# A gated recurrence over two layers on one core: two full-precision products made of rounded halves, span states in one group, work placed anew

## What is computed

```python
# layer 0
h = relu(x @ w1[lang] + b1[lang])                    # (1024, 128)
x = x + layernorm(x + h @ w2[lang] + b2[lang]) * gamma0[lang] + beta0[lang]
# layer 1
ctx    = causal_ema(x, tau_ctx)                      # h_t = alpha h_(t-1) + x_t
gated  = x * sigmoid(concat(x, ctx) @ Wg.T + bg)     # 1024 columns in, 512 out
h1     = gelu(x @ Wn1.T + bn1)
mod    = 0.5 + sigmoid(h1 @ Wn2.T + bn2)             # 8 values for each time step
traces = [causal_ema(gated * mod[..., d], tau_raws[d]) for d in range(8)]
temporal = sum_d traces[d] * softmax(blend)[d]
gate   = sigmoid(temporal @ Wtemp.T + btemp)
soma   = gelu(x @ Wsoma.T + bsoma)
x = x + layernorm((soma * gate) @ Wout.T) * gamma + beta
```

## Time and profile before

| | |
|---|---|
| profiled execution | 1546.37 us, span 1544.6 us, mean granted TensorE clock 0.988 |
| median of three runs | 1540.48 us |
| TensorE matmul busy | 1430.2 us, 93% of the span, 7532 records |
| VectorE busy | 1004.6 us, 65% |
| ScalarE busy | 466.4 us, 30% |
| GpSimd busy | 398.0 us, 26% |
| VectorE aggregates of one layer norm in a tile (L646, 4 instructions of 154 ns, and L648) | some 0.4 to 0.5 us from start to end |
| DMA | 186 MB, mean 121 GB/s |

### The profile page before, as it was taken

One profiled execution on the slowest core, in us unless ns is written; L12 is line 12 of the kernel. 1 busy time (PEld: TensorE's weight loads), 2 busy tenths in 40 slices (PEclk: granted clock), 3 DMA queues, 4 the chain that ended last, 5 costly groups with the idle time before them and its releaser, 6 DMA issues.

```text
span 1544.6 us, 18784 instructions
## 1 busy us (share of the span) xinstructions
PE 1430.2 (93%) x7532; PEld 911.1 (59%) x7532; DVE 1004.6 (65%) x1421; ACT 466.4 (30%) x723; POOL 398.0 (26%) x294
## 2 busy tenths in 40 slices
PE   2899999999999999999899998999999999999986
PEld 1555756566575655756566575655756566575643
DVE  6866666765766666666765766666666765766362
ACT  2323332332323323332332332323332332333321
POOL 4304132240422304232230422304132140421102
PEclk8899999999999999999999999999999999999998
DMA  6471542616236261452516344271542616243150
GB/s 209 165 194 55 152 122 91 189 48 170 83 116 168 80 162 55 147 160 90 156 42 181 112 120 133 79 193 55 149 124 89 191 43 176 83 121 97 54 138 28
DMA packets 66137, 186.18 MB, mean 121 GB/s; under 512 B 9090, under 2 KB 13826, under 8 KB 53762
## 3 DMA queue, kind: packets, MB, share of 16 engines
q1 hardware_dynamic: 66050, 184.97, 41.0%
HBM read 134.61 MB, written 50.33 MB: 120 GB/s over the span
## 4 chain that ended last, share of the span: by engine, by line
PE 34%; DMA 28%; DVE 23%; SPq 5%; issue 4%; ACT 2%; POOL 1%; POOLq 0%; DVEq 0%
DMA g_spans<-g 21%; PE ring L784 20%; PE ring L791 12%; DVE U L694 9%; DMA grep<-g_spans 6%; DVE x L676 6%; SPq L308 5%; DVE U L667 2%; DVE seq_lo L621 2%; PE Tp L922 1%; PE Tp L912 1%; DVE g L706 1%; DVE V L712 1%; ACT g L460 1%; DVE g L702 1%
## 5 line engine op out<-in xcount | busy, mean ns | idle before, releaser
L694 DVE TENSOR_TENSOR U<-grep,w_qs 128x1024 f32<-128x1024 f32 x256 | 297.6, 1220 | 116.3 <-DMA grep<-g_spans 116.0
L363 POOL TENSOR_TENSOR x<-grep,b_row 128x512 f32<-128x512 f32 x64 | 83.3, 1333 | 673.2 <-DMA grep<-in_x 673.2
L784 PE MATMUL ring<-Wout,soma 128*128 128x512 f32 x512 | 222.5, 593 | 3.0 <-DVE soma L627 3.0
L912 PE MATMUL Tp<-U,Arep 128*32 128x256 f32 x2048 | 151.8, 389 | 46.8 <-DVE U L694 46.2
L784 PEld LDWEIGHTS ring<-Wout,soma 128*128 128x128 f32 x512 | 97.1, 190 | 125.3 <-issue 121.5
L372 POOL TENSOR_TENSOR grep<-grep,beta_row 128x512 f32<-128x512 f32 x64 | 79.7, 1277 | 223.0 <-DMA grep<-x_tiles 223.0
L702 DVE TENSOR_TENSOR g<-ring,bg_row 128x512 f32<-128x512 f32 x64 | 44.1, 689 | 142.5 <-PE ring L791 80.5
L627 DVE TENSOR_TENSOR soma<-ring,soma 128x512 f32<-128x512 f32 x64 | 43.9, 686 | 141.3 <-ACT ring L421 141.3
L460 ACT ACTIVATE g<-g 128x512 f32<-128x512 f32 x64 | 40.4, 632 | 303.1 <-DVE g L702 303.1
L912 PEld LDWEIGHTS Tp<-U,Arep 128*32 128x32 f32 x2048 | 49.8, 108 | 134.6 <-DVE U L694 90.7
L791 PE MATMUL ring<-seq_hi,Wtemp_hi 128*128 128x512 f32 x256 | 107.3, 419 | 15.1 <-DVE seq_lo L621 15.1
(11 more groups left out here) (138 smaller groups left out, 2538.5 us busy)
## 6 DMA issues: line engine op xcount, KB each, us to landing
grep<-g_spans SPq DMA_DIRECT2D x256, 256.0 KB, 4.9
grep<-in_xc SPq DMA_DIRECT2D x16, 1024.0 KB, 5.3
grep<-in_x SPq DMA_DIRECT2D x16, 1024.0 KB, 5.8
x_tiles<-x SPq DMA_DIRECT2D x16, 1024.0 KB, 4.0
g_spans<-g SPq DMA_DIRECT2D x64, 256.0 KB
grep<-x_tiles SPq DMA_DIRECT2D x16, 1024.0 KB, 4.8
out<-U SPq DMA_DIRECT2D x64, 256.0 KB, 2.0
W<-in_w SPq DMA_DIRECT2D x16, 256.0 KB, 7.3
```

Source lines behind the costliest of these rows:

```text
L363: nc.gpsimd.tensor_tensor(new[:, b, :], x_t[:, b, :], b2_row[:, :], ALU.add).then_inc(xb2_ready, 1)
L694: V_.tensor_tensor(U[:, (n + 2) % 4, :, :], grep[b % 2][:, :, at], w_qs[:, hh, at].unsqueeze(1).to_broadcast([P, NI, HC]), ALU.mult).then_ ...
L784: last = nc.tensor.matmul(dst, lhsT(n), rhs(n), start=(n == 0), stop=(n == steps - 1))
L912: last = nc.tensor.matmul(Tp[b % 2][i * L:(i + 1) * L, at], Arep[:, b * NI + i, hh, :], U[:, (n + 2) % 4, i, :], start=(hh == 0 and c == 0 ...
```

## The change

- The y product (`hid` times `W2`) and the out product (`soma` times `Wout`) become `split_product`. So W2 is halved at each new language, Wout once, `hid` of layer 0 in each tile, and gated `soma` in each tile and quarter (ScalarE rounds behind VectorE's product, VectorE subtracts behind that). The remainder is written in the place of its original (`sb_two_ways` names the same memory twice); `soma_hi` lies in the memory of `g`, `hid_lo` and `hid_hi` in that of the two `T_sb`.
- `g` has 4 buffers. The span states of all 4 blocks are one group of four products behind `within_spans(0, 1)`, and one VectorE product forms `V`; `from_before` always reads 128 rows; `tile_state` is one product.
- soma 2 and soma 3 are halved on TensorE and put between other work. The transpositions of x1 come behind the last `from_before`, tt 2 and tt 3; those of channels 2 and 3 go to the `Tp` banks and leave the ring.
- SyncE asks for store 2 ahead of repeats 1, and for store 3 ahead of repeats 2; `keep_x1` stands at the end of the slot.
- VectorE's sums, statistics, centrings and updates are ordered anew; the x1 update stands ahead of the output's centring. Products of a block are ordered by piece.
- In the start the raw weights go where their remainders will lie, without staging buffers; GpSimd also forms Wout's remainder; VectorE's remainder of Wtemp comes behind `Arep`.

```diff
-        Wout = sb("Wout", [P, NC, C])
+        Wout_raw, Wout_lo = sb_two_ways("Wout", [P, NC, C])
+        Wout = [sb("Wout_hi", [P, NC, C], R), Wout_lo]
...
-        g = sb("g", [P, 2, C])
+        g, soma_hi = sb_two_ways("g", [P, NB, C])
...
+        def turned_bank(tile, n):
+
+            return bank_of("trx", tile, n) if n < 2 else Tp[3 - n]
...
                 def repeat_spans(b):
...
-                    sp.wait_ge(g_stored[b % 2], 16 * upto(2, k, b // 2))
+                    sp.wait_ge(g_stored[b], 16 * upto(1, k, 0))
                     if b >= 2:
                         sp.wait_ge(U_ready, upto(PIECES, k, 4 * (b - 2) + 3))
...
-                if has_next:
-                    sp.wait_ge(x1_stored, 16 * upto(1, k, 0))
-                    keep_x1(k + 1)
                 if has_cur:
                     store_spans(0)
                     repeat_spans(0)
                     store_spans(1)
+                    store_spans(2)
                     repeat_spans(1)
-                    store_spans(2)
                     store_spans(3)
                     repeat_spans(2)
                     repeat_spans(3)
+                if has_next:
+                    sp.wait_ge(x1_stored, 16 * upto(1, k, 0))
+                    keep_x1(k + 1)
...
-                def temporal_sigmoid(e):
+                def soma_gated(e):
                     ps = bank_of("temp", k - 1, e)
                     act.wait_ge(full["temp"], upto(4, k - 1, e))
                     nc.scalar.activation(ps[:, :], ps[:, :], ACT.Sigmoid, bias=col[:, 5 + e:6 + e]).then_inc(gate_ready, 1)
...
+                    act.wait_ge(sg_ready, upto(4, k - 1, e))
+                    nc.scalar.activation(soma_hi[:, e, :], soma[:, e, :], ACT.Identity).then_inc(somahi_ready, 1)
...
+                def soma_gated(e):
+                    dve.wait_ge(gate_ready, upto(4, k - 1, e))
+                    V_.tensor_tensor(soma[:, e, :], bank_of("temp", k - 1, e)[:, :], soma[:, e, :],
+                                     ALU.mult).then_inc(sg_ready, 1)
+                    dve.wait_ge(somahi_ready, upto(4, k - 1, e))
+                    V_.tensor_tensor(soma_lo[:, e, :], soma[:, e, :], soma_hi[:, e, :].bitcast(F),
+                                     ALU.subtract).then_inc(somalo_ready, 1)
...
+                if has_next:
+                    for b in range(NB):
+                        input_sum(b)
+                    input_statistics()
+                if has_prev:
+                    output_statistics(0)
+                if has_next:
+                    for b in range(NB):
+                        input_centred(b)
+                if has_prev:
+                    output_statistics(1)
                 if has_cur:
...
+                    context_low()
+                if has_prev:
+                    output_statistics(2)
+                if has_next:
+                    for b in range(NB):
+                        layer_input(b)
+                if has_prev:
+                    output_statistics(3)
+                    output_centred()
                 if k == 0:
...
+                    split(3)
...
-                        product(ps[:, :], lambda n: hid[:, b * P:(b + 1) * P], lambda n: W2[:, :], 1, "y")
-                if has_prev:
-                    pe.wait_ge(sg_ready, upto(4, k - 1, NC - 1))
...
+                        split_product(ps[:, :], lambda a, n: halves_of_h[a][:, b * P:(b + 1) * P],
+                                      lambda a, n: W2[a][:, :], 1).then_inc(full["y"], 1)
+                if has_prev:
+                    pe.wait_ge(somalo_ready, upto(4, k - 1, NC - 1))
...
-                        product(ps[:, :], lambda n: soma[:, n, b * P:(b + 1) * P], lambda n: Wout[:, n, :], NC, "out")
+                        split_product(ps[:, :], lambda a, n: gated[a][:, n, b * P:(b + 1) * P],
+                                      lambda a, n: Wout[a][:, n, :], NC).then_inc(full["out"], 1)
...
                     value_gate(2)
-                    span_states(0)
                     value_gate(3)
                     soma_of(1)
                     within_spans(0, 0)
                     within_spans(0, 1)
+                    span_states()
+                    soma_begun(2)
                     from_before(0)
-                    soma_of(2)
                     within_spans(1, 0)
+                    soma_ended(2)
                     within_spans(1, 1)
                     from_before(1)
-                    span_states(1)
                     trace_by_channels(0)
-                    soma_of(3)
                     within_spans(2, 0)
+                    soma_begun(3)
                     within_spans(2, 1)
                     from_before(2)
                     trace_by_channels(1)
+                    soma_ended(3)
+                    within_spans(3, 0)
                     if not odd:
                         tile_state()
-                    within_spans(3, 0)
+                    within_spans(3, 1)
+                    from_before(3)
                 if has_next:
                     x1_by_channels(0)
                 if has_cur:
-                    within_spans(3, 1)
-                    from_before(3)
                     trace_by_channels(2)
...
                     trace_by_channels(3)
                 if has_next:
+                    for n in range(1, NC):
+                        x1_by_channels(n)
```

More of the change, by code:

```diff
@@ L54, in sb, with sb_two_ways @@
             return ctx.enter_context(nc.sbuf_tensor(name, shape, dt))
+        def sb_two_ways(name, shape):
+            with nc.sbuf_tensor(f"{name}_f", shape, F) as plain:
+                pass
+            return plain, sb(f"{name}_r", shape, R)
         def bank(name):
@@ L162, in cond_resid_kernel @@
         setup_exp = sem("setup_exp")
-        split_lo = [sem(f"split_lo{n}") for n in range(5)]
+        split_lo = [sem(f"split_lo{n}") for n in range(6)]
         setup_step = sem("setup_step")
@@ L724, in slot @@
                     if k == 0:
-                        split(4, 1, [w[:, :, :] for w in Wtemp])
                         dve.wait_ge(setup_exp, 3)
```

364 lines of the change are left out of this document (198 added, 166 removed).

## The result

The changed kernel takes 1514.4 us (median; 1509.6 to 1521.2), the kernel before beside it 1541.2. The ratio is 0.983 [0.981, 0.984]: 27 us faster, where 58 were forecast. The time lies inside the wide range (1440 to 1516), above the forecast of 1462 to 1504 and among the times of rival 2 (1501 to 1518); the gain is under half of the forecast. The profiled execution is the fastest of the four: span 1507.8 and 1.75 around it. So span stands against span: 1544.6 - 1507.8 = 36.8 us. Of the four runs of the changed kernel the slowest (1521.2 us) has the lowest mean granted clock, 0.967, and the fastest (1509.6) the highest, 0.975; the two between (1513.9 and 1514.9) have 0.972 and 0.973.

A forecast was written before the change was run, and what follows sets the result against it. TensorE was taken to bound temporal start to z, a relay of g through DRAM the rest. 43 + 2 + 18 - 5 = 58 us off 1546.4 gave 1488, shifted to 1483 for the median; forecast 1462 to 1504, wide range 1440 to 1516.

The forecast's parts named there:

- rival 2: From z to the temporal product nothing gained or 1 us lost (1501 to 1518), or half clock (1510); chance 0.20.
- The products: From temporal start to z, rounded y and out products save 3.58 us a tile, 2.9 net; 43 in all.
- GpSimd's additions beside the remainders: Shared SBUF port: GpSimd's beta additions delay soma's last remainder, costing 0.7 us a tile, between nothing and 1.24.
- VectorE's order: Between temporal products and gate, reordered VectorE work makes z wait 0.3 to 0.6 us; its gain is almost nothing.
- The relay: From z (first modulation product) to the next temporal product, g's store and read-back: 1.1 us per tile, 18 in all.
- The queue on four engines: In the relay, g stores run on four DMA engines; store 2 delays repeats 1, block 2 gains 1.6 us, not 7.
- the one on the span states: After z, VectorE's span-state product (about 0.7 us) leaves the stretch; TensorE's restarts (some 0.3 us) fall into waits for U.
- Rival 1's floor: From z to temporal start TensorE reaches its floor, -4.4 us instead of -1.1 a tile: 53 more, 1430; chance 0.17.
- Rivals 3 and 4: 3: halves give back the products' 3.6 us, 1526 to 1541, chance 0.06. 4: later x1_back slows VectorE's row, 1549, chance 0.06.
- The start: In slot 0 TensorE waits longer for the second half of Wg's remainder: +5 us, bounds +2 and +8.
- the end: In the last slot no y product covers the halves: 2.9 - 1.3 = 1.6 us saved, counted as 2.

The follow-up runs named there:

- no_beta: The changed kernel without GpSimd's four beta 1 additions in each tile, so its output lacks beta: 1501.7 us.
- filler: The changed kernel with 12 more rounded products per tile where TensorE waits for V: 1504.2 us.
- v_early: The changed kernel with one line moved, so VectorE forms V ahead of block 1's first U: 1502.7 us.
- order_alone: The changed kernel with y and out in full precision again, without the halves of W2, Wout, hid and soma: 1556.2 us.
- v_early_late: The changed kernel with V formed ahead of block 1's first U and the beta 1 additions behind soma's last remainder: 1487.5 us.
- late: The changed kernel with GpSimd's beta 1 additions waiting for the last remainder of soma: 1505.0 us.
- wide_late: The changed kernel with g in DRAM in the order of its partitions and the beta 1 additions behind soma's last remainder: 1438.5 us.
- products_alone: The kernel before with the split products and their halves alone, its order of requests, span states and relay kept: 1509.8 us.

## Why the prediction was right in sign and wrong in size

**The products (43 forecast, 30 measured).** Two terms were mis-sized, and one stretch was miscounted. The raw saving is 3.08 us a tile where nothing disturbs (42.53 - 39.45, no_beta), not 3.58. Some 0.34 of the missing 0.50 can be placed: no_beta's first out product starts 0.46 us behind the last y product and the next one 0.34 behind that, where 0.23 is usual, though no wait is shown there:

```profile
769.66 0.40 PE L858 MATMUL ring<-W_hi,T_sb_r 128*128 128x512 f32 x1
770.12 0.50 PE L858 MATMUL ring<-Wout_hi,g_r 128*128 128x512 f32 x1
770.46 0.39 PE L858 MATMUL ring<-Wout_r,g_r 128*128 128x512 f32 x1
```

And GpSimd's additions beside the remainders cost 12.3 / 14 = 0.88 us a stretch, not 0.7. I had taken the middle between nothing and one GpSimd instruction of 1.24 us. The runs show no middle: eight stretches lose 1.36 us against no_beta and six lose 0.22. The rule of the Trainium skill that I had weighed (SBUF — State Buffer, "Who interferes with whom") has one of the two engines held for the other's whole instruction. The slow stretches agree with it: one addition takes 5.93 / 4 = 1.48 us there. The fifteenth stretch, in slot 15, has no y over the halves either, and I had booked 2.9 us for it all the same. TensorE waits 3.2 us for the last remainder there and 3.4 us of half clock follow: it lost 0.5 us (37.87 against 37.40), and without half clock, in no_beta, it gained 1.2.

**VectorE's order.** I expected z to wait 0.3 to 0.6 us for the GELU. GELU ends at 795.16 (ScalarE's row below) and z starts at 795.21, 0.28 behind the product before it, where 0.23 is usual: 0.05 at most. The gate's sigmoid is at z + 1.8 and store 0 at z + 3.2, where I had + 2.3 and + 3.8. The 3.9 us that I had read as two GELUs with a table load each are one load (1.28 us), two GELUs (0.69 and 0.68) and the load for the sigmoids (1.28), in the trace of the kernel before. The end of the first GELU came out right all the same, by luck; the gate's sigmoid did not. These misses were in my favour, and the sum had not charged the wait anyway.

```profile
794.47 0.69 ACT L485 ACTIVATE T_sb_f<-ring,columns 128x512 f32<-128x512 f32 x1
```

**The relay (18 forecast, 8 measured).** The queue on four engines was right, with blocks 1 and 2 up to 1 us earlier than forecast. 16 undisturbed stretches of 48.4 would be 774 us, 27 below the 801 of before, where 18 were forecast; filler (777.1) and v_early (777.2) come near them. The tiles with half clock took 19 of the 27 back. Their waits for V are also 4.5 us longer in sum than those of the tiles without, so up to 4 of the 19 may be waiting; 41 us at half clock, worth 20 at most, cover the rest. The step that failed is the one on the span states. The prediction says of their VectorE product only that it "leaves this stretch", and of "the single span-state group on TensorE" that its restarts "fall into its waits for U". I checked what the single V takes and not what it stands behind. It stands behind block 1's first U, which waits for repeats 1, and TensorE has nothing else to do. The half clock was in rival 2, with 27 us as its price and from a general reason, not from this place; about 19 came. The forecast needed one line more: in which place TensorE's waits come together into one.

**Rival 1's floor** (z to temporal start 4.4 us below before) was right to 0.1: with the other layout it is 45.56, 50.08 - 4.5. Only the change as made does not reach it. My average for before, 49.7, was itself 0.4 low, for the stretch from temporal start to z in slot 15 is 37.4 us and not 42.5.

**Rivals 3 and 4** did not come. The start (+5, measured +4.0) and the end (-2, measured -3.1) came within about 1 us; for the start that is partly luck, since first z scatters by as much. With the two one-line corrections the kernel takes 1487.5 us, close to the forecast of 1483. The nearness is in part luck as well. Temporal start to z falls by 41.9 us there (43 forecast, from a larger saving less a loss beside GpSimd) and z to temporal start by 24.7 (18 forecast), while first z comes 6.3 us later (5 forecast). What it does show is that two places of the order together cost 27 us.

## What to carry to other kernels

When an order is changed, list for every product that is merged or moved what stands ahead of it on its engine, and whether that waits for a transfer: here a wait of 3.8 us cost more than its length, since half clock came behind it. Before a relay through DRAM is reordered, look at how many DMA engines its store keeps busy; here the layout of one scratch tensor brought 62 us, more than twice what the whole change did. And where VectorE subtracts two operands in SBUF on the critical path, keep GpSimd's work out of that microsecond; here a single wait did it, for 9 us.

## What the runs showed of the hardware

- A wait of TensorE of 3.8 us was followed by 3.4 us at 1.2 GHz. So were all sixteen waits of 2.8 to 3.4 us in order_alone (at times with 6.8 us) and five of the eleven of 2.0 to 2.65 us in the changed kernel. But a wait of 3.2 us for the last remainder in slot 15 was followed by it in the changed kernel and not in no_beta or v_early_late. With nearly the same idle time in 76 pieces of at most 2.3 us, 17 us of half clock were left of 44.
- A store of 256 KB with 4 as its slowest dimension kept a quarter of the DMA engines busy and held its reader back for 5.88 us; with 128 it was up to 0.67 of them and 2.03 us. Repeats in pieces of 2 KB instead of 8 KB showed no cost in these kernels (4.4 us to landing against 5.0).
- A VectorE subtraction of 128x512 with both operands in SBUF took 0.69 us alone and 1.64 to 1.82 beside GpSimd's additions, one of which took 1.48 us there.
- It is not settled why first z scatters. In late, no_beta and wide_late it comes 1.3, 3.5 and 4.8 us after the changed kernel's 74.8, although the edits do not touch the start. So a difference of up to 5 us between two profiled executions can lie there; it bears on the 5 us between products_alone and the changed kernel, though there the intervals of the ratios lie apart.
